# Row maxima of an attention step turned, copied and sent one slot earlier, and sent as two transfers in place of one

## The chip, the cores and the metric

One NeuronCore of one Trainium2 chip runs the whole program. The metric is the device time of one execution in microseconds (us); several executions are timed and their median is taken.

## What is computed

The input x holds 16 samples of 128 rows and 256 columns. An attention over the columns (8 heads of 16 dimensions, queries, keys and values the same projection, with a mask) is followed by a layer of 8 small experts, of which each row takes its best one. Cut to what matters:

```python
q = xt @ Wq.T                                    # 16 samples, 256 positions, 8 heads x 16
scores = scale * einsum('bhqd,bhkd->bhqk', qh, qh)
logits = (scores * cmask + (1.0 - cmask) * NEG) * rmask
attn = softmax(logits, axis=-1)
out = (einsum('bhqk,bhkd->bhqd', attn, qh) ...) @ Wo.T
# expert layer: logits over 8 experts, the best one, weight from the two best
x = x + silu(gate) * up @ down, for the chosen expert, times its weight
```

## The kernel before

The program has two parts. The first is a pipeline over the 16 samples, written out by hand: the loop `for s in range(STEPS)` with `STEPS = B + 4 = 20` stands once in the code of each engine, and inside it `for h in range(NH)` makes eight slots. In step s each engine works on several samples at once. The second part gathers rows by expert and runs 23 tiles through the expert matrices.

In slot h of step s, TensorE (PE) computes the scores of sample s for the row maxima (`scores_for_max`, line 572, into bank 0 or 1) and the scores of sample s - 2 for the exponentials (`scores_for_exp`, line 584, into bank 2 or 3). VectorE (DVE) reduces the first to the row maxima (line 930). ScalarE (ACT) takes the exponential of the second (line 799). With two banks for each, the scores for the exponential of slot h wait until the exponential of slot h - 2 has been taken (`exp_done`), and those for the maxima until the reduction of slot h - 2 is done (`max_done`).

The matmul for the exponential must already subtract the row maximum. The kernel does that by a longer contraction: the tile `stack` holds on 96 partitions the three bf16 parts of q, on partition 96 (`ROW_MASK`) the mask and on partitions 97 and 98 (`ROW_MAX`) the row maxima of the sample, as two bf16 parts. So the maxima of a sample take this way through the engines, in step s for sample s - 1:

- GpSimd (POOL) splits them into two bf16 parts (`split_max`, lines 325 and 327).
- PE turns them with an identity (`turn_max`, line 563), in slot 2.
- DVE copies the result from PSUM to `max_rows` (`copy_max`, line 937), 32 partitions of 128 values, in slot 2 after the reduction of that slot.
- ACT issues the transfer from `max_rows` to the two rows of `stack` (`write_max`, line 827), in slot 3 after the exponential of that slot.
- In slot 0 of the next step `scores_for_exp` waits for it (`max_in`).

ACT issues other transfers as well: in slots 4 to 7, 0 and 1 it sends one of the six pieces of the right side of a later `stack` (line 437); SyncE (SP) sends the left side. Between them ACT copies the projected q (`copy_q`, line 784, slot 2), the values (slot 5), the products and the context. What an engine runs, and what it issues, goes in the order of its code.

The other PE work of a step is: the output projection in slot 0 (line 625), the products of probabilities and values in slots 1 and 6 (line 596), the projection of q in slot 2 (line 539), turns in slots 3 and 4 (606, 547) and the context with the router in slot 5 (line 617). Steps 13 to 15 have no projection of q; step 16 has no scores for the maxima.

Of the kernel before, what the change touches and what calls it, by code (L numbers as in the profile page):

```python
# [17 lines left out]
NH = 8  # L18
# [13 lines left out]
ROW_MAX = ROW_MASK + 1  # L32
ROWS2 = ROW_MAX + 2

NSTACK = 5
# [7 lines left out]
def adaln_ffn(nc, x, cond, wqT, woT, routerT, guT, dnT, out):  # L43
# [5 lines left out]
    NT = T // P  # L49
# [21 lines left out]
    with ctx:  # L71
        def sb(name, shape, dt=F32):
            return ctx.enter_context(nc.sbuf_tensor(name, shape, dt))
# [4 lines left out]
        def sems(name, n):  # L78
            return [sem(f"{name}{i}") for i in range(n)]
# [33 lines left out]
        stack = [sb(f"stack{r}", [P, 2, NH, T], BF16) for r in range(NSTACK)]  # L113
# [3 lines left out]
        max_rows = sb("max_rows", [2 * NH * NT, 2, P], BF16)  # L117
# [93 lines left out]
        max_in = sems("max_in", 2)  # L211
# [49 lines left out]
        def there(b):  # L261
            return 0 <= b < B
# [265 lines left out]
        def _(pe):  # L528
# [27 lines left out]
            def turn_max(b):  # L556
                pe.wait_ge(max_lo_made, b + 1)
                pe.wait_ge(v_copied, b + 1)
                if b == 0:
                    pe.wait_ge(consts_made, 3)  # L560
                    pe.wait_ge(zeros_made, 1)
                to = bank[VM][:, :].bitcast(BF16)
                t_.transpose(to[:, 0:P], max_parts[:, b % 2, :], ident_b[:, :]).then_inc(max_turned, 1)

            def scores_for_max(b, h):
                k, n = b % NSTACK, NH * b + h
                if h == 0:
                    pe.wait_ge(stack_in[k], 16 * 12 * (b // NSTACK + 1))
                if n >= 2:
                    pe.wait_ge(max_done, n - 1)  # L570
                for q in range(NT):
                    mm = t_.matmul(bank[h % 2][:, q * T:(q + 1) * T], stack[k][0:ROWS, 0, h, q * P:(q + 1) * P],  # L572
                                   stack[k][0:ROWS, 1, h, :], start=True, stop=True)
                mm.then_inc(s1_done, 1)

            def scores_for_exp(b, h):
                k, n = b % NSTACK, NH * b + h
                if h == 0:
                    pe.wait_ge(max_in[b % 2], 16 * (b // 2 + 1))
                    pe.wait_ge(mask_in[k], 16 * (b // NSTACK + 1))  # L580
                if n >= 2:
                    pe.wait_ge(exp_done, n - 1)
                for q in range(NT):
                    mm = t_.matmul(bank[2 + h % 2][:, q * T:(q + 1) * T], stack[k][0:ROWS2, 0, h, q * P:(q + 1) * P],  # L584
                                   stack[k][0:ROWS2, 1, h, :], start=True, stop=True)
                mm.then_inc(s2_done, 1)

            def apply_probs(b, g):
                pe.wait_ge(exp_done, NH * b + HG * (g + 1))
                if g == 0:  # L590
                    pe.wait_ge(v_copied, b + 1)
                    if b > 0:
                        pe.wait_ge(pv_copied, b)
                for k in range(NT):
                    for c in range(HG):
                        mm = t_.matmul(bank[PV][c * VC:(c + 1) * VC, g * T:(g + 1) * T], v_sb[:, b % NV, k, HG * g + c, :],  # L596
                                       probs[:, HG * g + c, k, :], start=(k == 0), stop=(k == NT - 1))
                mm.then_inc(pv_done, 1)
# [67 lines left out]
            for s in range(STEPS):  # L666
                for h in range(NH):
                    if there(s):
                        scores_for_max(s, h)
                    if there(s - 2):  # L670
                        scores_for_exp(s - 2, h)
                    elif s < 2:
                        keep_warm(2)
                    if h == 1 and there(s - 3):
                        apply_probs(s - 3, 1)
                    if h == 2:
                        if there(s - 1):
                            turn_max(s - 1)
                        if there(s + 3):
                            project_q(s + 3)  # L680
                        if s == B + 2:
                            table_early()
                    if h == 3 and s == B:
                        rank_early()
                    if h == 3 and there(s - 3):
                        turn_products(s - 3)
                        if s == B + 2:
                            keep_warm(3)
                    if h == 4 and there(s):
                        turn_values(s)  # L690
                    if h == 6 and there(s - 2):
                        apply_probs(s - 2, 0)
                    if h == 5 and there(s - 3):
                        turn_context(s - 3)
                        if s == B + 2:
                            keep_warm(2)
                    if h == 0 and there(s - 4):
                        project_out(s - 4)
# [74 lines left out]
        def _(act):  # L773
# [50 lines left out]
            def write_max(b):  # L824
                k = b % 2
                act.wait_ge(max_copied, b + 1)
                act.dma_start(stack[b % NSTACK][ROW_MAX:ROW_MAX + 2, 1, :, :], max_rows[:, k, :]).then_inc(max_in[k], 16)

            act.dma_start(wq_sb[:, :], wqT).then_inc(wq_in, 16)
            load_cond(act, 0)  # L830
# [16 lines left out]
            for s in range(STEPS):  # L847
                for h in range(NH):
                    if there(s - 2):
                        exponential(s - 2, h)  # L850
                    if h < 2 and s >= 1 and there(s + 1):
                        stack_part(act, s + 1, 1, h + 4)
                    if h == 1 and there(s - 4):
                        copy_hidden(s - 4)
                    if h == 1 and there(s - 3):
                        copy_products(s - 3)
                    if h == 2 and there(s + 3):
                        copy_q(s + 3)
                    if h == 3 and there(s - 1):
                        write_max(s - 1)  # L860
                    if h >= 4 and there(s + 2):
                        if h == 4:
                            need_parts(act, s + 2)
                        stack_part(act, s + 2, 1, h - 4)
                    if h == 5 and there(s - 4):
                        exp_gap(s - 4)
                    if h == 5 and there(s):
                        copy_v(s)
                    if h == 6 and there(s - 3):
                        copy_context(s - 3)  # L870
# [33 lines left out]
        def _(dve):  # L904
# [28 lines left out]
            def copy_max(b):  # L933
                dve.wait_ge(max_turned, b + 1)
                if b >= 2:
                    dve.wait_ge(max_in[b % 2], 16 * (b // 2))
                v.tensor_copy(max_rows[:, b % 2, :], bank[VM][:, :].bitcast(BF16)[0:2 * NH * NT, 0:P]).then_inc(max_copied, 1)

            def normalize(b):
# [210 lines left out]
            for s in range(STEPS):  # L1150
                for h in range(NH):
                    if there(s):
                        reduce_max(s, h)
                    if h == 1 and there(s - 4):
                        find_top(s - 4)
                        if s >= B:
                            find_best(s - 4)
                            mark_best(s - 4)
                            if s - 4 >= NE:
                                add_tokens(s - 4)  # L1160
                    if h == 2 and there(s - 1):
                        copy_max(s - 1)
                    if h == 2 and s == B + 1:
                        early_low(0, 4)
                        early_high()
                    if h == 2 and s == B + 2:
                        early_tokens()
                    if h == 3 and there(s - 3):
                        normalize(s - 3)
                    if h == 4 and there(s - 4) and s < B:  # L1170
                        find_best(s - 4)
                        mark_best(s - 4)
                    if h == 4 and s == B:
                        early_counts()
                        early_places()
                    if h == 4 and s == B + 1:
                        early_low(4, HOT)
                        find_experts(0, ET, edge[0:1, 1:E + 1])
                        not_early()
                    if h == 7 and there(s - 4):  # L1180
                        make_gate(s - 4)
# [56 lines left out]
```

## Time and profile before

| | |
|---|---|
| median of 3 runs | 226.68 us (225.11 to 228.05) |
| the profiled execution | 226.16 us, its span 224.3 us |
| granted TensorE clock, mean | 0.989 of full speed |
| PE busy | 208.8 us, 93% of the span |
| DVE, ACT, POOL busy | 65%, 60%, 51% |

The span is the time from the first to the last instruction of the profiled execution; the rest up to 226.16 us lies around it. The pipeline over the samples ends near 153 us, the expert part follows. A step of the pipeline takes 8.00 us in most steps and 7.53 us in steps without a projection of q. Times in the rows are us from the start of the span; "0.39 us x2" at a row of PE means two matmuls that overlap and end 0.39 us after the first began.

### The profile page before, as it was taken

What the parts mean: (1) busy time and instruction counts of PE and PEld (TensorE: products, weight loads), DVE (VectorE), ACT (ScalarE), POOL (GpSimd) and SP (SyncE); (2) the same over time, 40 slices, a digit from 0 to 9 for tenths busy, and PEclk for the clock granted to TensorE, in tenths of its full rate; (3) what the DMA queues carried; (4) which work ended last, traced back from release to release, by engine and by line L of the source; (5) the groups of instructions that cost most, each with busy time, mean ns of one, the idle gap of its engine ahead of it and who ended that gap; (6) DMA issues with size and microseconds to landing.
All of it is one profiled execution on the core that took longest, in us unless ns stands there. A gap on an engine that the chain in (4) does not pass through costs nothing.

```text
span 224.3 us, 5401 instructions
## 1 busy us (share of the span) xinstructions
PE 208.8 (93%) x1723; PEld 149.5 (67%) x1723; DVE 145.8 (65%) x403; ACT 133.5 (60%) x298; POOL 113.9 (51%) x212
## 2 busy tenths in 40 slices
PE   6997989999999989999999999988899999999970
PEld 5996757767657747757766775446677777777750
DVE  2886977789789879889788884674763223322330
ACT  2260378888778868888887788772543343334310
POOL 5782775366266346346421001304617777777752
PEclk9999999999999999999999999999999999999995
DMA  6795575879699697786865450002716654543210
GB/s 167 183 187 139 122 211 140 229 214 255 160 226 236 174 254 197 183 222 168 242 195 125 134 157 24 27 27 58 238 43 182 195 147 143 157 138 96 93 43 0
DMA packets 44987, 34.39 MB, mean 153 GB/s; under 512 B 6220, under 2 KB 42975, under 8 KB 44960
## 3 DMA queue, kind: packets, MB, share of 16 engines
q1 hardware_dynamic: 26896, 18.77, 32.1%
q10 hardware_dynamic: 15120, 7.04, 12.9%
q0 software_dynamic: 2944, 8.24, 12.6%
q8 instruction: 15, 0.25, 0.5%
q14 instruction: 12, 0.10, 0.1%
HBM read 16.91 MB, written 7.28 MB: 108 GB/s over the span
## 4 chain that ended last, share of the span: by engine, by line
PE 74%; DMA 8%; DVE 5%; SPq 4%; issue 3%; ACT 2%; POOL 1%; ACTq 1%; POOLq 1%; DVEq 0%
PE bank L572 13%; PE bank L596 12%; PE bank L718 12%; PE bank L584 11%; PE bank L737 4%; PE bank L739 4%; PE bank L617 3%; SPq L437 3%; PE bank L539 2%; PE bank L625 2%; PE bank L606 2%; PE bank L729 2%; DMA stack<-max_rows 2%; DMA stack<-parts 2%; PE bank L709 2%
## 5 line engine op out<-in xcount | busy, mean ns | idle before, releaser
L930 DVE TENSOR_REDUCE row_max<-bank 128x2 f32<-128x512 f32 x128 | 85.2, 684 | 12.0 <-PE bank L572 10.6
L799 ACT ACTIVATE probs<-bank 128x512 f32<-128x512 f32 x128 | 75.5, 598 | 21.4 <-PE bank L584 18.1
L572 PE MATMUL bank<-stack 96*128 96x256 bf16 x256 | 49.4, 274 | 2.6 <-DMA stack<-parts 1.6
L584 PE MATMUL bank<-stack 99*128 99x256 bf16 x256 | 48.3, 272 | 0.9 <-DMA stack<-max_rows 0.8
L572 PEld LDWEIGHTS bank<-stack 96*128 96x128 bf16 x256 | 20.5, 97 | 22.3 <-DVE row_max L930 10.9
L596 PE MATMUL bank<-probs,v_sb 128*32 128x256 f32 x512 | 34.3, 385 | 0.2 <-ACT probs L799 0.2
L305 POOL TENSOR_TENSOR qm<-q_sb,cond_all 128x256 f32<-128x256 f32 x15 | 10.9, 729 | 39.6 <-ACT q_sb L784 38.0
L718 PE MATMUL bank<-gu_sb,gotT 128*128 x92 | 31.0, 460 | 0.0
L584 PEld LDWEIGHTS bank<-stack 99*128 99x128 bf16 x256 | 24.1, 97 | 7.1 <-ACT probs L799 2.9
L554 PE MATMUL bank<-ident 128*128 128x128 f32 x148 | 21.2, 286 | 1.8 <-POOL ident L289 1.6
L596 PEld LDWEIGHTS bank<-probs,v_sb 128*32 128x32 f32 x512 | 13.4, 109 | 12.7 <-ACT probs L799 4.7
L554 PEld LDWEIGHTS bank<-ident 128*128 128x128 f32 x148 | 19.2, 200 | 2.5 <-POOL ident L289 1.6
L718 PEld LDWEIGHTS bank<-gu_sb,gotT 128*128 128x128 f32 x92 | 15.8, 190 | 4.9
L882 ACT ACTIVATE silu<-bank 128x176 f32<-128x176 f32 x23 | 7.3, 317 | 19.5 <-PE bank L718 19.5
L1188 DVE SCALAR_TENSOR_TENSOR act_sb<-silu,stack,bank 128x176 f32<-128x176 f32 x15 | 6.0, 398 | 19.7 <-ACT silu L882 19.7
L401 POOL DMA_INDIRECT out<-stack,put_i x15 | 14.9, 994 | 6.3 <-issue 3.7
L876 ACT COPY gotT<-bank 128x256 f32<-128x256 f32 x23 | 8.6, 373 | 14.9 <-PE bank L709 14.9
L392 POOL DMA_INDIRECT stack<-rows_dram,take_i x15 | 14.5, 967 | 4.6 <-issue 3.7
L392 POOL DMA_INDIRECT got<-rows_dram,take_i x8 | 7.9, 982 | 17.3 <-DVE take_i L1085 9.8
L737 PE MATMUL bank<-dn_sb,actT 128*128 x46 | 13.7, 380 | 0.0
L739 PE MATMUL bank<-dn_sb,actT 128*128 x46 | 13.7, 379 | 0.0
L955 DVE MAX8 top<-h_sb 128x8 f32<-128x8 f32 x16 | 2.7, 170 | 15.2 <-ACT h_sb L818 15.2
(160 smaller groups left out, 316.5 us busy)
## 6 DMA issues: line engine op xcount, KB each, us to landing
stack<-parts SPq DMA_DIRECT2D x96, 64.0 KB, 3.0
stack<-parts ACTq DMA_DIRECT2D x96, 64.0 KB, 3.1
gu_sb<-in_guT SPq DMA_DIRECT2D x8, 352.0 KB, 3.9
rows_dram<-h_sb SPq DMA_DIRECT2D x16, 132.5 KB, 2.3
x_sb<-in_x SPq DMA_DIRECT2D x16, 128.0 KB, 3.7
rows_dram<-in_x SPq DMA_DIRECT2D x4, 512.0 KB, 5.2
cond_all<-in_cond SPq DMA_DIRECT2D x12, 128.0 KB, 4.7
dn_sb<-in_dnT SPq DMA_DIRECT2D x4, 256.0 KB, 3.9
```

Source lines behind the costliest of these rows:

```text
L305: g.tensor_tensor(qm[:, k, :], q_sb[:, b % NQ, :], cond_all[:, b % NCOND, :], ALU.mult).then_inc(qm_made, 1)
L392: g.indirect_dma_start(home(n, 0, ROW), None, rows, bass.IndirectOffsetOnAxis(ap=take_i[:, n:n + 1], axis=0)).then_inc(got_in[n], 16)
L401: g.indirect_dma_start(out_rows, bass.IndirectOffsetOnAxis(ap=put_i[:, n:n + 1], axis=0), home(n, XROW, ROW), None, bounds_check=TOK - 1, ...
L554: t_.matmul(bank[3][:, 0:P], ident[:, :], ident[:, :], start=True, stop=True)
L572: mm = t_.matmul(bank[h % 2][:, q * T:(q + 1) * T], stack[k][0:ROWS, 0, h, q * P:(q + 1) * P], stack[k][0:ROWS, 1, h, :], start=True, stop ...
L584: mm = t_.matmul(bank[2 + h % 2][:, q * T:(q + 1) * T], stack[k][0:ROWS2, 0, h, q * P:(q + 1) * P], stack[k][0:ROWS2, 1, h, :], start=True ...
L596: mm = t_.matmul(bank[PV][c * VC:(c + 1) * VC, g * T:(g + 1) * T], v_sb[:, b % NV, k, HG * g + c, :], probs[:, HG * g + c, k, :], start=(k ...
L718: mm = t_.matmul(bank[1 + m2][:, 0:I2], gotT[:, m2, k, :], gu_sb[:, k, bass.ds(e, 1), :].rearrange("p a i -> p (a i)"), start=(k == 0), st ...
L737: t_.matmul(bank[4 + m2][:, 0:T], actT[:, m2, 0, :], dn_sb[:, bass.ds(e, 1), :].rearrange("p a t -> p (a t)"), start=True, stop=False)
L739: t_.matmul(bank[4 + m2][:, 0:T], actT[:, m2, 1, :], dn2_sb[:, bass.ds(e, 1), :].rearrange("p a t -> p (a t)"), start=False, stop=True).th ...
L799: a.activation(probs[:, h, :, :].rearrange("p k t -> p (k t)"), bank[2 + h % 2][:, 0:NT * T], ACT.Exp, scale=float(DK) ** -0.5).then_inc(e ...
L930: v.tensor_reduce(row_max[:, b % 2, h, :], bank[h % 2][:, 0:NT * T].rearrange("p (q k) -> p q k", q=NT), AX.X, ALU.max).then_inc(max_done, 1)
```

## The change

Three calls move up by one slot: PE turns the maxima in slot 1 in place of slot 2, DVE copies them in slot 1, ACT issues the transfer in slot 2, after the copy of q, in place of slot 3 after the exponential. The one transfer of 32 pieces becomes two: one for each of the two rows of `stack`, each of sixteen pieces of 256 bytes, and both add to the same semaphore, so that its waits count 32 for each sample.

```diff
                 if h == 0:
-                    pe.wait_ge(max_in[b % 2], 16 * (b // 2 + 1))
+                    pe.wait_ge(max_in[b % 2], 32 * (b // 2 + 1))
...
                     if h == 1 and there(s - 3):
                         apply_probs(s - 3, 1)
+                    if h == 1 and there(s - 1):
+                        turn_max(s - 1)
                     if h == 2:
-                        if there(s - 1):
-                            turn_max(s - 1)
...
                 act.wait_ge(max_copied, b + 1)
-                act.dma_start(stack[b % NSTACK][ROW_MAX:ROW_MAX + 2, 1, :, :], max_rows[:, k, :]).then_inc(max_in[k], 16)
+                for part in range(2):
+                    act.dma_start(stack[b % NSTACK][ROW_MAX + part:ROW_MAX + part + 1, 1, :, :].rearrange("p h (q t) -> p (h q) t", q=NT),
+                                  max_rows[part * NH * NT:(part + 1) * NH * NT, k, :]).then_inc(max_in[k], 16)
...
-                    if h == 3 and there(s - 1):
+                    if h == 2 and there(s - 1):
                         write_max(s - 1)
...
-                    dve.wait_ge(max_in[b % 2], 16 * (b // 2))
+                    dve.wait_ge(max_in[b % 2], 32 * (b // 2))
...
-                    if h == 2 and there(s - 1):
+                    if h == 1 and there(s - 1):
                         copy_max(s - 1)
```

On ACT, slots 2 and 3 of a step in the middle of the pipeline (L784 is the copy of q, L799 the exponentials, L437 the first piece of `stack` in slot 4; the lines of the change have a new number):

```order
 L799 ACTIVATE probs<-bank 128x512 [waits s2_done]
 L784 COPY q_sb<-bank 128x256 [waits v_done,q_done]
-L799 ACTIVATE probs<-bank 128x512 [waits s2_done]
-L827 DMA stack<-max_rows 2x16x128 [waits max_copied]
+L828 DMA stack<-max_rows 1x16x128 [waits max_copied]
+L828 DMA stack<-max_rows 1x16x128
+L799 ACTIVATE probs<-bank 128x512 [waits s2_done]
 L799 ACTIVATE probs<-bank 128x512 [waits pv_done,s2_done]
 L437 DMA stack<-parts 16x8x256 [waits s2_done,parts_made]
```

The exponential of slot 3, which stood ahead of the one transfer, now stands behind both.

On PE, the end of slot 1 and slot 2 of the same step (L563 is the turn of the maxima, L539 the projection of q):

```order
 L596 MATMUL bank<-probs,v_sb 32x256 [waits exp_done]
 L596 MATMUL bank<-probs,v_sb 32x256 x7
-L572 MATMUL bank<-stack 128x256 [waits max_done]
-L572 MATMUL bank<-stack 128x256
-L584 MATMUL bank<-stack 128x256 [waits exp_done]
-L584 MATMUL bank<-stack 128x256
-L563 MATMUL bank<-ident_b,max_parts 128x128 [waits v_copied,max_lo_made]
+L563 MATMUL bank<-ident_b,max_parts 128x128 [waits v_copied,max_lo_made]
+L572 MATMUL bank<-stack 128x256 [waits max_done]
+L572 MATMUL bank<-stack 128x256
+L584 MATMUL bank<-stack 128x256 [waits exp_done]
+L584 MATMUL bank<-stack 128x256
 L539 MATMUL bank<-x_sb,wq_sb 128x256 [waits q_copied,x_in2]
```

The turn moved ahead of the four score matmuls of slot 2; the projection of q stays behind them.

## Rows read from the trace of the kernel before

**Rows 1.** Busy us (count) of PE, PEld, DVE, ACT, POOL; clock, DMA share, GB/s

```profile
67.48:75.48 8.00, 8.00 (x81) 5.53 (x79) 6.96 (x18) 6.79 (x15) 4.31 (x10) 1.00 0.82 210
75.48:84.41 8.93, 8.17 (x82) 5.46 (x79) 6.96 (x18) 6.68 (x15) 4.31 (x10) 1.00 0.95 232
```

**Rows 2.** Timeline of PE in step 7: start us, us, engine, line

```profile
75.03 0.39 PE L572 MATMUL bank<-stack 96*128 96x256 bf16 x2
...
75.48 0.22 PE L563 MATMUL bank<-ident_b,max_parts 128*128 128x128 bf16 x1
75.54 0.65 PE L539 MATMUL bank<-x_sb,wq_sb 128*128 128x256 f32 x2
...
76.25 0.38 PE L584 MATMUL bank<-stack 99*128 99x256 bf16 x2
...
77.79 0.38 PE L584 MATMUL bank<-stack 99*128 99x256 bf16 x2
...
80.25 0.38 PE L584 MATMUL bank<-stack 99*128 99x256 bf16 x2
80.61 0.38 PE L572 MATMUL bank<-stack 96*128 96x256 bf16 x2
```

**Rows 3.** Timeline of ACT, POOL and DVE in step 7; ACTq is ACT issuing

```profile
73.50 0.22 POOL L327 TENSOR_TENSOR max_parts<-row_max,max_parts 128x16 bf16<-128x16 f32 x1
...
75.21 0.17 DVE L955 MAX8 top<-h_sb 128x8 f32<-128x8 f32 x1 [0.61 <-ACT h_sb L818]
...
76.22 0.37 ACT L784 COPY q_sb<-bank 128x256 f32<-128x256 f32 x1
...
76.67 0.60 ACT L799 ACTIVATE probs<-bank 128x512 f32<-128x512 f32 x1
76.67 0.68 ACTq L827 DMA_DIRECT2D stack<-max_rows  x1
```

**Rows 4.** Timeline: one transfer that is not waited for, and the wait in step 8

```profile
68.68 0.67 ACTq L827 DMA_DIRECT2D stack<-max_rows  x1
...
72.83 0.38 PE L584 MATMUL bank<-stack 99*128 99x256 bf16 x2
...
81.75 0.39 PE L584 MATMUL bank<-stack 99*128 99x256 bf16 x2 [0.76 <-DMA stack<-max_rows]
```

**Rows 5.** Timeline of ACT and ACTq: a pair of issues, and a long one

```profile
24.61 1.25 ACTq L437 DMA_DIRECT2D stack<-parts  x2
...
57.39 1.54 ACTq L437 DMA_DIRECT2D stack<-parts  x1
...
58.97 0.38 ACT L818 COPY h_sb<-bank 128x264 f32<-128x264 f32 x1 [0.99 <-issue]
```

**Rows 6.** Instructions that touch stack: durations of an issue in ns, min/median/max

```profile
L437 ACTq DMA_DIRECT2D stack<-parts x96: 552/574/1537, 5.8 to 122.7; - x96
...
L827 ACTq DMA_DIRECT2D stack<-max_rows x16: 622/671/1203, 22.1 to 139.3; - x16
```

**Rows 7.** DMA issues of the page: KB each, median us to landing

```profile
stack<-parts ACTq DMA_DIRECT2D x96, 64.0 KB, 3.1
```

**Rows 8.** Timeline of step 13, without a projection of q

```profile
116.73 1.10 ACT L799 ACTIVATE probs<-bank 128x512 f32<-128x512 f32 x2
...
118.35 0.38 PE L584 MATMUL bank<-stack 99*128 99x256 bf16 x2
```

**Rows 9.** Timeline of step 16, the last with row maxima

```profile
139.30 0.62 ACTq L827 DMA_DIRECT2D stack<-max_rows  x1
...
140.08 0.60 PE L584 MATMUL bank<-stack 99*128 99x256 bf16 x4
...
141.05 0.73 PE L617 MATMUL bank<-turn_rt,ctx_sb 128*128 128x136 f32 x4 [0.37 <-DVE ctx_sb L946]
```

**Rows 10.** Timeline of steps 2 and 3, where the pipeline fills

```profile
27.23 0.10 PEld L563 LDWEIGHTS bank<-ident_b,max_parts 128*128 128x128 bf16 x1 [0.32 <-POOL max_parts L327]
...
32.44 0.39 PE L572 MATMUL bank<-stack 96*128 96x256 bf16 x2 [0.64 <-ACT probs L799]
```

## The prediction

> **What bounds the kernel now.** I read the page first, then busy time by stretch, then the timelines of single steps, and last the list of waits. In a plain step of 8.00 us PE is busy for 8.00 us, at the full 2.4 GHz clock, DVE for 6.96 and ACT for 6.79 us [rows 1]. So PE sets the length of a step and the other two have about one us of slack, but in an order in which PE waits for both. The next step of the list, 75.48 to 84.41, takes 8.93 us for the same work. What ended last there is the transfer of the row maxima: it was issued at 76.67, and the scores that need it began at 81.75, after 0.76 us of idle PE [rows 3, 4]. The same pair of rows one step earlier shows 68.68 and 72.83, 4.15 us apart, with no wait [rows 4]. The list of waits names this transfer once, so one step of them all lost time to it, 8.93 - 8.00 = 0.93 us [rows 1]. That is all that a faster or earlier transfer can win in the profiled execution.
>
> **What moves at no cost.** The split maxima are ready at 73.72 [rows 3], and the turn now stands where the scores of slot 2 begin, at 75.03 [rows 2]: no wait there. It takes as much of PE before these scores as it took after them. The projection of q stays behind them, so it and the copy of q keep their times. On DVE the copy of 0.2 us goes between the search of the best expert, which ends at 75.21 + 0.17 = 75.38 [rows 3], and the reduction of slot 2, which waits for scores that begin at 75.03 + 0.06 and take 0.39 [rows 2]: some 0.1 us, covered by what DVE waits for anyway. Both are done before ACT comes to the transfer at 76.2. GpSimd and SyncE keep their order.
>
> **What the ACT queue pays.** This is the main term. Before, ACT gave out the exponential of slot 3 at 76.67 and issued the transfer while it ran [rows 3]; the issue was over at 77.35, when the exponential had just ended, so it was hidden. Now two issues stand ahead of that exponential. An issue holds what is queued behind it: the one of 1.54 us that began at 57.39 let the next copy start only at 58.97, with 0.99 us of idle ACT put down to issue [rows 5]. Issuing can start when the copy of q has been given out, at 76.22 [rows 3]. For the length of the pair there are two bounds: two pieces of stack in a row take 1.25 us and the shortest single one 0.552, while the transfer of the maxima took 0.671 in the median against 0.574 for a piece of stack [rows 5, 6]. So a pair takes 1.21 us (2 x 0.58 + 0.05) to 1.39 us (2 x 0.67 + 0.05). I take 1.27, nearest to the pair in the rows, since the new transfers have half the pieces of the old one.
>
> The exponential of slot 3 then starts at 76.22 + 1.27 + 0.02 = 77.51 in place of 76.67 and ends 0.60 later, at 78.11. The scores of slot 5 need its bank. They began at 77.79 [rows 2], 0.52 us after the old end; now they begin 0.04 after the new one, at 78.15: 0.36 us late. DVE does not wait for this and catches up. That matters at the end of the step: the last scores for an exponential began at 80.25 and the first of the next step at 80.61, where the pitch of such a pair in the same step is 0.22, so 0.14 us were a wait for DVE [rows 2], which the delay now covers. A plain step grows by 0.36 - 0.14 = 0.22 us. ACT has room for it: it idles for 8.00 - 6.79 = 1.2 us in a step [rows 1], more than the 0.84 by which the exponential is late, so nothing is carried into the next step.
>
> **The sum.** Steps 3 to 12 are ten plain steps: 10 x 0.22 = 2.2 us. In steps 13 to 15 there is no copy of q: ACT gives out the exponential of slot 2 near 116.8, the pair ends at 118.07, the exponential at 118.69, and the scores of slot 5, at 118.35 before [rows 8], start at 118.73: 0.38 us, with no wait at the end of the step to cover it, 3 x 0.38 = 1.14 us. In step 16 the copy on DVE stands behind the same expert search as before, so the first issue is still at 139.30. Before, the exponential of slot 3 ran beside it; now it follows at 140.59 and ends at 141.19. The scores of slot 5, the second pair of the four matmuls from 140.08, slip to 141.23, and the context behind them from 141.05 to 141.45 [rows 9]: 0.40 us. In step 2 PE already waited 0.32 us for the split maxima, until 27.23 [rows 10]; one slot earlier it waits longer for them, 0.40 us of lost time, and the pair adds 0.36; but at 32.44 PE stood idle for 0.64 us in front of step 3 [rows 10] for pieces of stack that come as before, so of 0.76 some 0.1 us is left. Together 2.2 + 1.14 + 0.40 + 0.1 = 3.84 us.
>
> Against it stands the wait of 0.93 us. The first row of maxima leaves 0.44 us earlier than before (76.23 for 76.67), the second 0.2 us later, and the scores that need them come 0.22 us later. A transfer of parts, eight times as large, lands 3.1 us after its issue in the median [rows 7], the old one of the maxima took 5.0 in step 7. I take the wait as gone. 226.16 + 3.84 - 0.93 = 229.07, so **229.1 us** for an execution like the profiled one. This is also my median: 226.16 lies 0.52 under the median of 226.68, but the lowest time, 225.11, is what the profiled one would be without its wait (225.23), which suggests that this wait is a part of the spread, and without it the spread is smaller. That is 1.1% above 226.68.
>
> The Trainium skill, page "DMA: Bandwidth & Descriptors", section "Why a DMA increments its semaphore by 16 and not by 1", says that a transfer uses as many of the 16 engines as divide the slowest dimension above one of both sides. By that rule the old shape (2 rows against 32) ran on two engines and each new one (16 against 16) on all sixteen, and the wait would go; if it does not hold for this shape, the sum keeps the 0.93. The trace of before shows only the late landing, not the engines.
>
> **The rivals.**
>
> *The exponential is not held.* If the pair took 0.9 us or less, the exponential of slot 3 would end before 77.75 and PE would lose nothing: only the wait goes, 226.16 - 0.93 = 225.2 us. For it speaks the slack of 0.52 us, against it that none of the 96 issues of this kind on ACT was under 0.552 us [rows 6].
>
> *The transfers land no earlier.* Sixteen pieces and two landings to wait for, with the second issued later than the old one was; in a step as full as 75.48 to 84.41, with a DMA share of 0.95 [rows 1], both may be late. Then the wait of 0.93 stays: 226.16 + 3.84 = 230.0 us.
>
> *The issues stretch: slower.* An issue on ACT is 0.57 us in the median, but 1.20 and 1.54 happened [rows 5, 6]. Before, a long issue of the maxima was covered by the exponential beside it; now every us of it is a us of PE, since the exponential has no slack left behind the pair. Slower by over 2% begins at 231.2 us, 2.1 above the forecast. Over 14 steps that is 0.15 us a step, a mean pair of 1.42 us, just over the upper bound of 1.39. With pairs of 1.5 us it is 229.07 + 14 x 0.23 = 232.3 us. For it speaks that the two new transfers go out back to back in the part of a step in which SyncE issues too; against it that 1.25 is seen for pairs.
>
> The same page's section "Rules for kernel authors" advises to join many small transfers into one, as they are mostly overhead. The trace agrees in so far as a piece of 64 KB and the 8 KB of the maxima cost ACT about the same to issue [rows 6]. By that rule the second transfer is a pure addition and this rival or the forecast is the way it goes.
>
> *The wait was worth more.* If most timed executions held several such waits, their end could win more than the pair costs. The span from 225.11 to 228.05 allows three at most; even then the time would be near 226, and below 222.1 only if the exponential is not held either.
>
> **How the numbers follow.** A measurement of this kernel can tell about 2% from no change, that is 222.1 to 231.2 us. Chances: forecast 0.45 (228.3 with pairs of 1.21 us, 230.8 with 1.39), exponential not held 0.17 (225.2), landing no earlier 0.18 (230.0; 231.7 with the longer pair), issues stretched 0.17 (232.3 and up), worth more 0.03. All but the fourth end within 2%, save for a little of the third and, below, most of the last. Faster 0.03, same 0.79, slower 0.18. The range runs from 225.0 to 232.3 us: it leaves out half of the stretched case and the last one.
>
> **What would show it.** The profile after should have: no PE idle put down to the maxima; the two issues behind the copy of q, 1.2 to 1.4 us together; the exponential of slot 3 about 0.84 us later in its step; PE idle of 0.3 to 0.4 us before the scores of slot 5, released by ACT; plain steps of 8.2 us and late ones of 7.9. The prediction is wrong if the exponential starts while the issues run, if plain steps stay at 8.00 us, or if the issues are far from the bounds.

## The result, and the profile after

The change makes the kernel slower: 231.37 us in the median of 4 runs (230.34 to 231.83) against 227.37 us before (4 runs, 225.11 to 229.28), a ratio of 1.021 with a 95% interval from 1.016 to 1.026. The forecast was 229.1 us, 1.1% up, with a range of 225.0 to 232.3 us; the measured time lies in the range, and its interval holds the 2% at which the prediction began to call a time slower. The profiled execution took 231.83 us with a span of 229.9 us, 5.6 us more than the 224.3 us before.

The 5.6 us lie in the pipeline. From the turn of the maxima in step 3 to that in step 16 are 109.39 us, before 103.79. Busy time by step, with columns as in [rows 1]:

```profile
42.85:52.43 9.58, 8.15 (x83) 5.40 (x80) 7.13 (x17) 6.62 (x15) 4.61 (x10) 1.00 0.79 205
78.30:87.23 8.93, 8.15 (x83) 5.40 (x79) 7.03 (x17) 6.58 (x15) 4.33 (x10) 1.00 1.01 234
87.23:96.20 8.97, 7.97 (x83) 5.47 (x80) 7.11 (x17) 6.57 (x15) 4.35 (x10) 1.00 0.82 227
96.20:104.34 8.14, 7.97 (x83) 5.47 (x80) 7.02 (x17) 6.61 (x15) 3.86 (x9) 1.00 0.71 177
120.76:128.47 7.71, 7.54 (x81) 5.17 (x78) 6.38 (x17) 6.07 (x13) 0.83 (x4) 1.00 0.65 165
```

PE has the same work as before (7.97 us in a plain step, at the full clock), but no step with a projection of q is at 8.00 us any more. The last two rows are the quiet cases: 8.14 us with a projection of q and 7.71 without, where it was 8.00 and 7.53. The first three take up to 1.6 us more than 8.00.

A quiet step, the timeline of ACT and then of PE in the changed kernel:

```profile
97.35 0.55 ACTq L828 DMA_DIRECT2D stack<-max_rows  x1
97.40 0.37 ACT L784 COPY q_sb<-bank 128x256 f32<-128x256 f32 x1
97.93 0.61 ACTq L828 DMA_DIRECT2D stack<-max_rows  x1
98.58 0.60 ACT L799 ACTIVATE probs<-bank 128x512 f32<-128x512 f32 x1 [0.82 <-PE bank L584]
...
99.24 0.39 PE L584 MATMUL bank<-stack 99*128 99x256 bf16 x2 [0.17 <-ACT probs L799]
```

The pair of issues lasts from 97.35 to 98.54, 1.19 us, beside the copy of q. The exponential of slot 3 starts 0.04 us after its end and ends at 99.18; the scores of slot 5 start at 99.24. The row puts the idle time of ACT down to PE's scores; that is the releaser seen last, but those scores had long been done, and the exponential starts where the issues end. This is the mechanism of the forecast, with a wait of 0.17 us at its end.

The step before it, same view, with a long second issue:

```profile
88.38 0.55 ACTq L828 DMA_DIRECT2D stack<-max_rows  x1
88.44 0.37 ACT L784 COPY q_sb<-bank 128x256 f32<-128x256 f32 x1
88.97 1.43 ACTq L828 DMA_DIRECT2D stack<-max_rows  x1
90.44 0.60 ACT L799 ACTIVATE probs<-bank 128x512 f32<-128x512 f32 x1 [1.64 <-PE bank L584]
...
91.10 0.39 PE L584 MATMUL bank<-stack 99*128 99x256 bf16 x2 [1.00 <-ACT probs L799]
```

Here the second issue takes 1.43 us in place of 0.61, the exponential starts at 90.44, and PE is idle for 1.00 us. The first issue of a pair is 0.55 us in most steps (0.51 to 0.57), the second is 0.61 us in seven of the steps 3 to 15 and 0.83, 1.26, 0.82, 0.82, 1.43 and 0.73 us in the other six. Short pairs take 1.19 us, the mean pair 1.36 us.

The trace holds more on the long ones. SyncE issues transfers of its own in this part of a step, and the timeline of step 4 shows the two beside each other:

```profile
44.19 1.65 SPq L481 DMA_DIRECT2D rows_dram<-in_x  x1
44.59 1.26 ACTq L828 DMA_DIRECT2D stack<-max_rows  x1
```

Both are long, and both end at 45.84 or 45.85. The issue of 1.43 us ends at 90.40, one of SyncE's that took 0.97 us at 90.41. The other four long ones began 0.03 to 0.18 us after an issue of SyncE and ended 0.25 to 0.31 us after its end. Of the seven short ones, three had no issue of SyncE running when they began, three began 0.39 us or more after one of SyncE's, and the seventh began 0.03 us before one, which then took 0.86 us. So the long issues go with issues of SyncE beside them; no run takes those away, so this isn't shown to be the cause.

The group of these scores in the page of the changed kernel:

```profile
L584 PE MATMUL bank<-stack 99*128 99x256 bf16 x256 | 48.5, 273 | 7.0 <-ACT probs L799 5.7
```

The list of waits (us in all, times, longest):

```profile
PE bank L584 <- ACT probs L799: 5.7, 14, 1.0
...
PE bank L584 <- DMA stack<-max_rows: 1.0, 2, 0.6
```

The instructions of the line that issues, with durations in ns (min/median/max):

```profile
L828 ACTq DMA_DIRECT2D stack<-max_rows x32: 510/602/1428, 21.6 to 145.3; - x32
...
DMA to landing us min/median/max: 1.6/2.8/5.6
```

And the two waits for the maxima in the timeline of PE:

```profile
50.22 0.39 PE L584 MATMUL bank<-stack 99*128 99x256 bf16 x2 [0.61 <-DMA stack<-max_rows]
...
85.02 0.39 PE L584 MATMUL bank<-stack 99*128 99x256 bf16 x2 [0.40 <-DMA stack<-max_rows]
```

The scores waited 0.9 us in all before, now 7.0, of which 5.7 for the exponential. And the wait for the maxima, one of 0.76 us before [rows 4], is not gone: there are two, of 0.61 and 0.40 us.

### The profile page after: what moved, and what is told of

The parts are those of the page before. It is cut to its first block, busy times and chain, and to the rows that moved or that the text cites. A ratio compares the mean times of both kernels' runs of the same rounds, so it can differ in the third digit from the quotient of the medians.

```text
span 229.9 us, 5417 instructions
## 1 busy us (share of the span) xinstructions
PE 209.2 (91%) x1723; PEld 148.7 (65%) x1723; DVE 146.9 (64%) x403; ACT 132.6 (58%) x298; POOL 114.1 (50%) x212
## 4 chain that ended last, share of the span: by engine, by line
PE 60%; ACT 11%; issue 7%; ACTq 7%; DMA 6%; POOL 5%; DVE 2%; POOLq 1%
PE bank L718 11%; PE bank L596 11%; PE bank L584 8%; ACT probs L799 7%; ACTq L828 6%; PE bank L572 6%; DMA stack<-max_rows 5%; PE bank L737 4%; PE bank L739 4%; PE bank L554 4%; ACT pv_sb L806 3%; PE bank L617 3%; PE bank L729 2%; PE bank L625 2%; PE bank L709 2%
## 5 line engine op out<-in xcount | busy, mean ns | idle before, releaser
L799 ACT ACTIVATE probs<-bank 128x512 f32<-128x512 f32 x128 | 74.3, 597 | 29.0 <-PE bank L584 24.0
L584 PEld LDWEIGHTS bank<-stack 99*128 99x128 bf16 x256 | 22.7, 97 | 17.2 <-ACT probs L799 12.7
L572 PEld LDWEIGHTS bank<-stack 96*128 96x128 bf16 x256 | 22.7, 98 | 13.1 <-DVE row_max L932 5.8
```

The costliest lines, as they stand in the source:

```text
L799: a.activation(probs[:, h, :, :].rearrange("p k t -> p (k t)"), bank[2 + h % 2][:, 0:NT * T], ACT.Exp, scale=float(DK) ** -0.5).then_inc(e ...
```

## The experiments

Ratios are to the kernel before on the same chip, with 95% intervals; "the pipeline" is the time from the turn in step 3 to the turn in step 16 (103.79 us before, 109.39 us after). The diffs are cut to the lines that tell the variant from the others; every trace is of one execution.

**The move alone.** The turn, copy and issue moved as in the change, one transfer of 32 pieces as before.

```diff
-                    if h == 3 and there(s - 1):
+                    if h == 2 and there(s - 1):
                         write_max(s - 1)
```

> Turn, copy and issue moved up as in the change, but the transfer stays one of 32 pieces. Held queue (my theory: the exponential of slot 3 waits behind the issues, and the scores of slot 5 wait for it): one issue of 0.67 us ends 0.6 us earlier than the pair did, the exponential of slot 3 starts some 0.25 us late and ends before the scores of slot 5 want its bank (0.52 us of slack), so no idle PE there, plain steps of 8.00 us, and a time of 226 to 227.5 us, ratio 0.995 to 1.003, save for steps in which the issue stretches. Rival A (it is the second transfer as such, wherever it is issued): the same time as before, and e2 as slow as the change. Rival B (the moved turn and copy cost): most of the 4 us of loss is here, 230 to 231 us.

Ratio 1.000 [0.997, 1.004], profiled 225.6 us, pipeline 102.60. ACT and PE in the timeline of step 7:

```profile
76.13 0.68 ACTq L827 DMA_DIRECT2D stack<-max_rows  x1
...
76.85 1.19 ACT L799 ACTIVATE probs<-bank 128x512 f32<-128x512 f32 x2 [0.30 <-PE bank L584]
...
77.68 0.38 PE L584 MATMUL bank<-stack 99*128 99x256 bf16 x2
```

The same step by busy time:

```profile
76.00:84.00 8.00, 7.97 (x81) 5.48 (x80) 6.98 (x18) 6.65 (x15) 4.31 (x10) 1.00 0.84 219
```

The single issue stands ahead of the exponential too and holds it to its end, 76.81, but the scores of slot 5 don't wait and the step stays at 8.00 us. A hold of 0.67 us is inside the slack; one of 1.19 us is not. No step waits for the maxima. Its profiled execution is 0.56 us shorter than the one before, which had its one wait of 0.76; the ratio of the runs shows nothing of that.

**The split alone.** Two transfers, turn, copy and issue in the slots of before.

```diff
-                act.dma_start(stack[...][ROW_MAX:ROW_MAX + 2, 1, :, :], max_rows[:, k, :]).then_inc(max_in[k], 16)
+                for part in range(2):
+                    act.dma_start(stack[...][ROW_MAX + part:ROW_MAX + part + 1, 1, :, :]..., max_rows[part * NH * NT:..., k, :]).then_inc(max_in[k], 16)
```

> Two transfers as in the change, but turn, copy and issue in their old slots, the issues behind the exponential of slot 3. Held queue: the pair runs beside the exponential, from 76.7 to 77.9 in the step of the rows; the exponential of slot 4 starts 0.4 us late, 0.1 us before the scores of slot 6 want its bank, so short pairs cost nothing and stretched ones (1.4 to 2.0 us) 0.2 to 0.8 us each: 227 to 229 us, ratio 1.00 to 1.01. Rival A (second transfer as such): 230 to 231.5 us, as the change. Rival B (turn and copy): as before, 226.5 to 227.5 us.

Ratio 1.018 [1.011, 1.025], pipeline 107.03: a miss of the held-queue theory as I had put it (1.00 to 1.01). The list of waits:

```profile
PEld bank L584 <- DMA stack<-max_rows: 3.7, 6, 1.3
...
PE bank L584 <- DMA stack<-max_rows: 2.0, 4, 1.0
```

The timeline of ACT and PE in step 4:

```profile
43.75 2.46 ACTq L828 DMA_DIRECT2D stack<-max_rows  x2
...
46.31 0.60 ACT L799 ACTIVATE probs<-bank 128x512 f32<-128x512 f32 x1 [1.97 <-issue]
...
46.97 0.39 PE L584 MATMUL bank<-stack 99*128 99x256 bf16 x2 [1.02 <-ACT probs L799]
```

Plain steps are at 8.00 us, so in the old slot a short pair is hidden, as expected. But the second row leaves 0.6 us later and four steps wait for the maxima, 2.0 us in all; and one pair of 2.46 us pokes out of its cover and costs PE 1.02 us. Six of the 13 pairs take 1.31 us or more here too. Its long issue, 1.88 us from 44.34, ends at 46.22, as does one of SyncE's that took 1.39 us. By the ratio the split alone costs nearly as much as the change, with intervals that overlap; of the 5.6 us of the pipeline this trace shows 3.2, by other waits.

**Turn and copy alone.** Both moved, transfer as before in its slot.

```diff
-                    if h == 2 and there(s - 1):
+                    if h == 1 and there(s - 1):
                         copy_max(s - 1)
```

> Only the turn on PE and the copy on DVE moved up; one transfer, issued in slot 3 behind the exponential as before. Held queue and rival A: no difference, 226.5 to 227.5 us, ratio 0.997 to 1.003, steps of 8.00 us, the issue at the same place in the step. Rival B: 230 to 231 us.

Ratio 1.006 [1.001, 1.011], above the 0.997 to 1.003 expected; profiled 225.88 us, pipeline 103.57 against 103.79. Plain steps take 8.00 us. One step of 9.2 us holds an issue of `stack` pieces (line 437) of 2.60 us, which this edit doesn't touch; at its end the scores wait for the exponential behind it (0.83 us) and their weight load for the maxima (1.09 us), which end within 0.1 us of each other. The move of these two is free in the steps of the trace; where the 0.6% of the runs lies isn't seen.

**One issue, ahead of the copy of q as well.** Turn and copy moved; the one transfer issued in slot 2 before the copy.

```diff
+                    if h == 2 and there(s - 1):
+                        write_max(s - 1)
                     if h == 2 and there(s + 3):
                         copy_q(s + 3)
-                    if h == 3 and there(s - 1):
-                        write_max(s - 1)
```

> Turn and copy moved up, one transfer, issued in slot 2 between the exponential of slot 2 and the copy of q, where ACT waits 0.5 us for the projection of q. Held queue: the issue (0.67 us) runs beside the exponential of slot 2 and ends about when the copy of q could start, so at most 0.1 us a step is lost, the transfer leaves 1 us earlier than before and the waits for it go: 225 to 226.5 us, ratio 0.990 to 0.998. Rival A: the same. Rival B: 229 to 231 us. If waits for the transfer were no part of the time of before, 226.5 to 227.5 us.

Ratio 1.008 [1.003, 1.012], pipeline 105.26, plain steps 8.31 to 8.33 us: a miss. ACT in step 7:

```profile
76.98 0.68 ACTq L827 DMA_DIRECT2D stack<-max_rows  x1
...
77.78 0.37 ACT L784 COPY q_sb<-bank 128x256 f32<-128x256 f32 x1 [0.21 <-issue]
78.05 1.28 ACT L799 ACTIVATE probs<-bank 128x512 f32<-128x512 f32 x2
```

The same issue that was free behind the copy costs 0.3 us a step ahead of it, but not by the exponential. Counted from the turn of the step (76.26 here, 74.98 in the move alone), the exponential of slot 3 starts after 1.79 us, with the move alone after 1.87, and the scores of slot 5 are on time in both. It is the copy of q that is late, at 1.52 us in place of 1.20. GpSimd waits for it, and DVE meets GpSimd's later work. GpSimd, DVE and PE in this kernel:

```profile
79.50 0.67 POOL L312 TENSOR_TENSOR rest<-qm,parts 128x256 f32<-128x256 f32 x1
79.52 0.66 DVE L959 TENSOR_TENSOR gap<-top 128x1 f32<-128x1 f32 x1
...
81.48 0.39 PE L572 MATMUL bank<-stack 96*128 96x256 bf16 x2 [0.20 <-DVE row_max L930]
```

and in the move alone:

```profile
77.89 0.67 POOL L312 TENSOR_TENSOR rest<-qm,parts 128x256 f32<-128x256 f32 x1
78.23 0.34 DVE L959 TENSOR_TENSOR gap<-top 128x1 f32<-128x1 f32 x1
...
79.92 0.39 PE L572 MATMUL bank<-stack 96*128 96x256 bf16 x2
```

In both, DVE's operation on a single column ends within 0.01 us of GpSimd's, and it takes 0.66 us here in all eight full steps, 0.34 there. The reductions behind it start 0.32 us later, and the scores for the maxima that need them 0.28 us later, which is the loss. No step waits for the maxima, but that wins far less than this costs.

**Two transfers that are always issued one way.** The order of the change, with the old transfer of 32 pieces and the same once more to a tile that nobody reads (an extra transfer).

```diff
+                act.dma_start(spare[:, k, :, :], max_rows[:, k, :]).then_inc(max_in[k], 16)
```

> Order of the change, with two transfers of the old shape in place of the two halves: the first is the real one of 32 pieces, the second copies the same 32 pieces to a spare tile that nothing reads, and the waits count both. Held queue: a pair of 1.39 us in front of the exponential of slot 3, so PE waits 0.35 to 0.4 us before the scores of slot 5, plain steps of 8.2 to 8.4 us, 2.5 to 4.5 us slower than before (ratio 1.011 to 1.020). Theory L: in addition no waits for the maxima, and few stretched issues, as with one transfer. Theory S: waits for the maxima and stretched issues as often as in the changed kernel, ratio 1.02 or more.

Ratio 1.031 [1.022, 1.040], pipeline 109.27. Timeline of ACT and PE in a step:

```profile
79.17 0.68 ACTq L828 DMA_DIRECT2D stack<-max_rows  x1
...
79.88 0.67 ACTq L829 DMA_DIRECT2D spare<-max_rows  x1
80.59 0.60 ACT L800 ACTIVATE probs<-bank 128x512 f32<-128x512 f32 x1 [1.01 <-PE bank L585]
...
81.25 0.39 PE L585 MATMUL bank<-stack 99*128 99x256 bf16 x2 [0.36 <-ACT probs L800]
```

The durations of the second issue, of the extra transfer:

```profile
L829 ACTq DMA_DIRECT2D spare<-max_rows x16: 621/671/707, 23.5 to 146.0; - x16
```

The pair is 1.38 us in nearly every step, PE waits 0.35 to 0.40 us in steps 3 to 14, and plain steps take 8.32 us. With the move alone this gives three sizes of one cost: 0.67 us of issues ahead of the exponential, 0.00 us a step; 1.19 us, 0.15; 1.38 us, 0.33. The second issue never stretched here (0.707 at most), while six of 13 did in the change. The list of waits has one row more:

```profile
PE bank L585 <- DMA spare<-max_rows: 1.2, 2, 0.9
```

Two steps wait for the second transfer, 0.35 and 0.85 us, nearly as in the change, though it has the old shape. Theory L puts the waits down to the shape of sixteen pieces, theory S to the second issue and its place. Neither holds whole: the waits are there, which L had excluded, and the stretching isn't, which S wanted; and the ratio is above the 1.011 to 1.020 of the held queue. The pipeline is as long as the change's, 109.27 and 109.39 us, of other parts: a longer hold in each step and no stretched issues.

**Is it the traffic of the expert weights?** The changed kernel with the loads of the expert weights behind the pipeline; only its steps are read, since the second part then waits for them.

```diff
-                if 0 <= s - 2 < N_EXPERT_DMAS:
-                    load_experts(s - 2)
...
+            for i in range(N_EXPERT_DMAS):
+                load_experts(i)
```

> The changed kernel with the 14 loads of expert weights issued behind the pipeline over the samples, so that their 3.3 MB do not meet the transfers of the pipeline; the whole time grows since the expert part then waits for them, and only the steps are to be read. Theory H+L (a held exponential costs 0.15 us in each step, and stretched issues and late landings, which come from busy DMA queues, make the rest): plain steps of 8.1 to 8.2 us, second issues of 0.61 us save for one or two, no wait for the maxima or one, and 3 us or more of the 5.6 us lost in the pipeline come back. Rival (stretches come from SP and ACT issuing at once, whatever is in the queues): as many stretched issues as in the changed kernel, 6 or 7 of 16 pairs over 1.25 us.

The pipeline takes 107.62 us, so 1.8 of the 5.6 us came back, less than the 3 expected. One wait for the maxima is left, 0.91 us. Second issues of 0.83, 0.78 and 1.26 us are still there in steps 3 to 15, three of 13 in place of six; the one of 1.26 us ends within 0.01 us of one of SyncE's of 1.65 us. The weights' traffic is not needed for either loss. Whether it makes them more frequent, one execution can't tell.

**Does spreading make the maxima land earlier?** The kernel before, issuing the one transfer two slots later (run twice), the two halves two slots later, and one half at its time and the other two slots later. In all of them the scores come soon after the issue, so the landing shows as a wait.

```diff
-                    if h == 3 and there(s - 1):
+                    if h == 5 and there(s - 1):
                         write_max(s - 1)
```

> The kernel before with its one transfer issued two slots later, in slot 5 behind the exponential, 2.6 us ahead of the scores that need it, so that PE waits in each step and the landing can be read. It is made to be slower. Theory L (sixteen engines land later under load, because the last of sixteen busy queues decides): the one transfer of the old shape lands 2 to 3 us after its issue, waits of 0 to 0.8 us a step, and 3 us or more only in a few steps. Theory S (only the second issue and its place matter, the shape does not): the landing is the same as that of each half in the split kernel beside it.

> The same kernel as e5, run beside e9, so that the two are compared on one chip: 229 to 231.5 us, waits for the maxima in three to seven steps of 0.3 to 1.3 us.

> The same place in slot 5, with the two transfers of sixteen pieces. Theory L: each lands 0.5 to 1.5 us later after its own issue than the one transfer does, with a spread up to 5 us where the DMA share is near one; waits of PE 1 to 2.5 us a step. Theory S: the second lands 0.6 us after where the one transfer lands, since it is issued 0.6 us later, so the waits grow by 0.6 us a step over the kernel with one transfer, to the tenth.

> Split transfers with turn and copy in their old slots: the half for the second row goes out alone in slot 3, where the old transfer did, and the half for the first row alone in slot 5, where e5 issued its one transfer of 32 pieces. So one single transfer of sixteen pieces stands in the place of e5, with nothing issued directly ahead of it. Theory L (the shape on sixteen queues lands late under load): waits of PE for it in most steps, 0.5 to 1.5 us each, pipeline 4 us or more longer than in e5. Theory S (only the second issue behind the first makes the lateness of e6): steps as in e5, with waits in five steps or so.

The waits of PE for the maxima, of the late one, the late one again, and the late half:

```profile
PE bank L584 <- DMA stack<-max_rows: 3.9, 5, 1.3
```

```profile
PE bank L584 <- DMA stack<-max_rows: 5.9, 6, 1.7
```

```profile
PE bank L584 <- DMA stack<-max_rows: 7.7, 5, 2.6
```

From issue to scores, where they waited: 3.62, 3.79, 3.03, 4.03 and 3.24 us for the one transfer; 3.22, 3.26, 3.87, 4.31, 4.46 and 3.39 us in its second run; 4.75, 3.73, 4.11, 3.79 and 4.47 us for the late half; 4.38, 3.23, 3.95, 3.78 and 3.69 us from the second issue of the late pair (and 2.36 us once behind the last sample). So the sixteen pieces land no earlier. The means, 3.66 us of eleven and 4.17 us of five, stand the other way, but the ranges overlap: whether a lone half lands later stays open. The pipeline is 108.09 and 110.85 us with the one transfer late and 116.27 with the half late; that is the 4 us or more that theory L asked for against its run, but part of it is a clock that fell after the waits of PE (0.92, 0.92 and 0.87 in three steps of the half, 0.86 in one of the second run), so I don't count it as shown. The whole times (230.39, 233.37, 244.12 and 238.17 us, one run each) compare no better. The second run of the late one missed its forecast of 229 to 231.5 us: two runs of one kernel differ by 3 us here. Lone halves hardly stretched: one of the 28 of steps 3 to 16 took 0.75 us. In the late pair it was the first issue that stretched, to 0.83, 1.07, 1.08 and 1.55 us in four steps.

**The issue on another queue.** Turn and copy moved; GpSimd issues the one transfer in place of ACT.

```diff
+                pool.wait_ge(max_copied, b + 1)
+                g.dma_start(stack[...][ROW_MAX:ROW_MAX + 2, 1, :, :], max_rows[:, k, :]).then_inc(max_in[k], 16)
```

> Turn and copy moved up, the one transfer of 32 pieces issued by GpSimd, which waits for the copy of q there anyway, in place of ACT. ACT loses one issue of 0.67 us a step, which ran beside an exponential. If ACT issues cost the kernel only where they hold an exponential that PE waits for: plain steps stay at 8.00 us and the stalls behind long issues of stack pieces get a little shorter, 225.5 to 227 us, ratio 0.993 to 1.001. If the transfer leaves or lands later from GpSimd: waits for the maxima in several steps, ratio 1.005 to 1.03.

Ratio 1.012 [1.004, 1.021]; the median is 228.58 us, the profiled execution 226.49. A step of its profile by busy time:

```profile
76.00:84.00 8.00, 7.96 (x82) 5.47 (x81) 6.96 (x18) 6.68 (x15) 4.98 (x12) 1.00 0.87 229
```

Its list of waits, where GpSimd comes to the issue:

```profile
POOL stack L355 <- DVE max_rows L936: 32.5, 16, 2.7
```

In the profile the pipeline is shorter than before (102.19 us) and no scores wait for the maxima, at the price of GpSimd standing 2.0 us a step. Four of its six runs are at 228.4 to 229.0 us all the same, and the profiled execution is one of the two short ones; where those four lose is not seen. No version is faster than the kernel before.

## Why the prediction was right in its direction and short in its size

**The queue of ACT, main term: mechanism right.** The issues hold the exponential of slot 3, it starts 0.04 us behind them, the scores of slot 5 wait for it, and no delay is carried on. It is shown by taking one issue away (cost 0.00) and by making the pair 1.38 us long (cost 0.33). The term was 0.22 us a step for a pair of 1.27 us; it is 0.15 for one of 1.19. The two parts of it can be read: the scores of slot 5 come 3.04 us after the turn, with the move alone 2.70, so 0.34 us late (0.36 was forecast), and at the end of the step 0.19 us of that are covered (0.14 was forecast). Between a hold of 1.19 and of 1.38 us the step grows as fast as the hold, as the working had it. For steps 13 to 15 the forecast was 0.38; the one with a short pair and nothing else, step 13, grew by 0.18, step 15 by 0.35, and step 14 by 0.46 behind a long issue of `stack` pieces. In step 16 the scores of slot 5 waited 0.69 us, of which some 0.35 us are new; 0.40 was forecast. For short pairs the whole term is 10 x 0.15 + 3 x 0.2 + 0.35 = 2.5 us, where 3.84 was forecast.

**The length of the pair: the term that was mis-sized.** I took 1.27 us "nearest to the pair in the rows" and put 1.21 and 1.39 as its bounds. The short pairs are below that, but six of 13 are 1.31 to 2.02 us, for their second issues are longer by 0.22 + 0.65 + 0.21 + 0.21 + 0.82 + 0.12 = 2.2 us than 0.61, and each of those us is one of PE, in step 9 for example 8.97 - 8.15 = 0.82. That is the rival "the issues stretch", which named the mean pair from which it decides, 1.42 us; it was 1.36, so the case came out between this rival and the forecast. The trace of before had the row for it, with issues of 1.20 and 1.54 us [rows 5, 6]; my error was to price one of them as a rare event.

**"I take the wait as gone": the step that failed.** The forecast took 0.93 us off. Two steps still wait, and they are longer than short or stretched pairs explain by 9.58 - 8.15 - 0.65 = 0.78 and 8.93 - 8.15 - 0.21 = 0.57 us, 1.35 us together: the term is +0.4, not -0.93. This was the rival "the transfers land no earlier". The forecast gave the earlier start of the first row as its reason, but both transfers must land. The second left later than the old one had; the late variants show that a half of sixteen pieces lands no sooner than the whole, and two transfers of the old shape were waited for as well. So it is the second transfer, and not its shape, that brings the waits: in four traces with two transfers PE waited for the maxima in 2, 4, 1 and 2 steps (the change, the split alone, no weights between, two of the old shape), in five with one transfer at its old time or earlier once (before). The move alone had no such wait in its profile, so the move could have won these 0.9 us where they occur, and the split gave them away.

By the Trainium skill, page "DMA: Bandwidth & Descriptors", section "Why a DMA increments its semaphore by 16 and not by 1", the new shape goes over all sixteen engines and the old over two. The runs don't show the engines, only that the landing did not become shorter. The advice of its section "Rules for kernel authors" to join many small transfers into one agrees with what was measured: the second transfer cost 0.61 us of ACT or more and bought nothing.

**What was free.** Turn and copy were, in steps of 8.00 us with them moved. "The exponential is not held" is refuted by every step of the profile after.

**The sum again.** 2.5 (hold) - 0.35 (step 16, behind the last turn) + 2.2 (stretch) + 0.4 (maxima) + about 0.7 for long issues of `stack` pieces (1.95 us at 59.04, where before had 1.54 at 57.39 [rows 5], and 1.05 at 127.58) = 5.45 us, where the pipeline grew by 5.60. The last term is scatter between executions, not shown to be the change's. In the prediction's terms: the hold was put 1.3 us too high (3.84 for 2.5), the stretch 2.2 and the maxima 1.3 us too low (-0.93 for +0.4). That the time still fell in the range owes something to luck, since the first error covers part of the others.

**What stays open.** Why the issues stretch. It needs neither the weights' traffic nor the second place in a pair (first issues did it in the late pair), and the shape alone doesn't do it (lone halves hardly do), nor two issues in a row alone (the pairs of 32 pieces don't). The rival that the traces favour is issuing by SyncE at the same time; the longest issues end together with one of SyncE's, that of 1.54 us in the kernel before too (58.93 and 58.92). But no run moves SyncE's issues, and one long issue of the late pair (1.55 us) had none beside it. Open as well is where the issue on GpSimd loses outside its profile.

## What to carry to other kernels

An issue in the queue of a compute engine was free here behind the instruction that the bottleneck waits for, as long as it ended before the next one was wanted (a pair of 2.46 us did not). Ahead of it, it costs what goes beyond the slack: read the slack between the end of that instruction and its consumer, here 0.52 us, and count the issues against it. Do so for every consumer: ahead of the copy of q the same issue cost 0.3 us a step by way of GpSimd and DVE. To split a small transfer doubles its issues and sends its last part later, so ask first whether the whole one is slow for a reason that splitting removes. And where a trace shows a few long issues, price them at how often they come, by the queue they would now hold.

## What was not expected of the hardware

- An issue of sixteen pieces of 256 bytes took ACT 0.55 us, one of 32 pieces 0.67 us: not the half, so two halves cost 1.8 times the whole.
- The second issue of a pair took 0.61 us or, in six of 13 steps, 0.73 to 1.43 us; in the kernel with the split alone one pair took 2.46 us. The longest end within 0.01 us of an issue of SyncE that was long as well.
- From issue to the scores that waited for them, 4 to 8 KB took 3.0 to 4.8 us in the late variants, while the median landing was 2.1 and 2.4 us in the two of them for which the trace has landings: the waits are made by the tail, which a median doesn't show.
- DVE's operation on one column took 0.34 us or 0.66 us, as it began beside the later or the earlier part of an operation of GpSimd, and ended with it in both.
